# Front blocks' numbers by loads of six registers, group 6 loaded behind its own count, and some orders of work changed

## The reference

```python
x = x + _L0_xattn_ref(_layernorm(x), ctx, ctx, ...)   # softmax cross attention, 16 heads of 8, 77 keys
x = x + _L0_ffn_ref(_layernorm(x), ...)               # 8 experts, top 2, silu(x W1 + b1) * (x W2 + b2), W3
x = x + _L1_xattn_ref(_layernorm(x), ctx, ...)        # linear attention: softmax of q and k over features
x = x + _L1_ffn_ref(_layernorm(x), ...)               # 8 experts, top 2, gelu(x W1 + b1) W2, plus 2 shared experts
```

## Time and profile before

| what | value |
|---|---|
| median of 3 runs | 716.31 us (714.04 to 717.26) |
| profiled execution | 716.5 us |
| its span | 714.5 us |
| PE busy | 655.3 us (92%) |
| DVE, POOL, ACT busy | 452.1, 383.2, 340.4 us (63, 54, 48%) |
| mean DMA rate | 128 GB/s; 250 to 278 GB/s in most of the two routed parts |
| stages | attention 0 to about 243; routed 0 from 260 to 387; attention 1 to 558; routed 1 from 559 to 697; tail to 714.5 |

### The profile page before, as it was taken

How to read it: one execution, slowest core, us unless ns; L and a number is a source line. 1 busy time by engine, 2 the same in 40 slices (tenths; PEclk the granted TensorE clock), 3 DMA queues, 4 the chain that set the end, 5 groups by cost and what they waited for, 6 DMA issues and landing times.

```text
span 714.5 us, 15805 instructions
## 1 busy us (share of the span) xinstructions
PE 655.3 (92%) x5160; PEld 494.1 (69%) x5160; DVE 452.1 (63%) x1336; ACT 340.4 (48%) x739; POOL 383.2 (54%) x502
## 2 busy tenths in 40 slices
PE   6999999999998879999998899999998799999991
PEld 3556666665667669899997455556554599999990
DVE  2577788788877757786778568776564133333433
ACT  3444454454443244444666466766543354544440
POOL 5312255765746744555677566676645145545552
PEclk9999999999999689999999999999999999999997
DMA  6831112112210167888882300000001888888875
GB/s 178 238 61 11 8 20 30 34 19 29 36 26 24 55 174 220 248 260 265 253 262 84 100 31 27 23 30 27 31 21 52 237 272 261 264 261 268 278 232 165
DMA packets 102120, 91.36 MB, mean 128 GB/s; under 512 B 52952, under 2 KB 85848, under 8 KB 101720
## 3 DMA queue, kind: packets, MB, share of 16 engines
q1 hardware_dynamic: 88487, 69.85, 35.4%
q0 software_dynamic: 8640, 17.84, 7.1%
q10 hardware_dynamic: 4913, 2.67, 1.4%
HBM read 69.14 MB, written 22.72 MB: 129 GB/s over the span
## 4 chain that ended last, share of the span: by engine, by line
PE 65%; DVE 14%; SPq 5%; issue 5%; ACT 4%; DMA 3%; POOL 2%; POOLq 0%; DVEq 0%; ACTq 0%
PE pair L1543 37%; PE pair L1877 11%; PE pair L1546 8%; PE pair L1941 5%; DVE sm L1272 4%; DVE smax L1268 4%; PE pair L1668 2%; PE pair L1683 2%; DMA xr<-xs_sorted 1%; SPq L500 1%; SPq L504 1%; POOL xs_sorted L615 1%; SPq L493 1%; ACT L924 1%; SPq L494 1%
## 5 line engine op out<-in xcount | busy, mean ns | idle before, releaser
L689 POOL DMA_INDIRECT y_tok<-ysb,xr x142 | 138.8, 978 | 123.7 <-DVE ysb L1149 58.5
L615 POOL DMA_INDIRECT xs_sorted<-xa,slot_i x128 | 131.5, 1027 | 86.2 <-DVE slot_i L1055 50.9
L1543 PE MATMUL pair<-xT,w_all 128*128 128x256 f32 (+1 forms) x640 | 139.3, 362 | 0.0
L1543 PEld LDWEIGHTS pair<-xT,w_all 128*128 128x128 f32 x640 | 109.7, 196 | 9.6
L1877 PEld LDWEIGHTS pair<-w_all,hT 128*128 128x128 f32 x852 | 107.6, 194 | 6.0 <-issue 2.8
L1877 PE MATMUL pair<-w_all,hT 128*128 128x128 f32 x852 | 109.3, 277 | 2.2 <-DVE hT L1135 1.9
L873 ACT ACTIVATE hT<-pair,w_all 128x256 f32<-128x256 f32 (+1 forms) x160 | 62.5, 448 | 74.5 <-PE pair L1543 73.8
L1127 DVE COPY xT<-pair 128x256 f32<-128x256 f32 (+1 forms) x80 | 31.4, 393 | 95.2 <-PE pair L1546 91.5
L937 ACT ACTIVATE hS<-pair,w_sh 128x512 f32<-128x512 f32 x64 | 44.0, 687 | 60.5 <-PE pair L1543 59.7
L1543 PE MATMUL pair<-xeT_all,w_sh 128*128 128x512 f32 x128 | 68.6, 619 | 0.0
L1941 PE MATMUL pair<-hS,w_sh 128*128 128x512 f32 x128 | 66.4, 602 | 0.0
(11 more groups left out here) (222 smaller groups left out, 1090.3 us busy)
## 6 DMA issues: line engine op xcount, KB each, us to landing
w_all<-in_w SPq DMA_DIRECT2D x40, 578.0 KB, 4.3
w_all<-in_w SPq DMA_DIRECT2D x40, 450.0 KB, 3.9
xa<-y_tok SPq DMA_DIRECT2D x32, 256.0 KB, 4.3
xr<-xs_sorted SPq DMA_DIRECT2D x62, 130.0 KB, 3.3
y_tok<-ysb,xr POOLq DMA_INDIRECT x142
xs_sorted<-xa,slot_i POOLq DMA_INDIRECT x128, 2.3
xs_sorted<-in_pads SPq DMA_DIRECT2D x12, 130.0 KB, 3.9
xr<-xs_sorted SPq DMA_DIRECT2D x18, 65.0 KB, 2.6
```

Source lines behind the costliest of these rows:

```text
L615: g.indirect_dma_start(xs_dram[l], bass.IndirectOffsetOnAxis(ap=slot_i[:, i:i + 1], axis=0), xa[:, GT * c + j // TOPK, j % TOPK, :], None)\
L689: g.indirect_dma_start(y_dram[l], bass.IndirectOffsetOnAxis(ap=xr[u % NXR][:, t, P:P + 1].bitcast(I32), axis=0), ysb[u % NYB][:, t, :], None)\
L1543: return mm(out_, l_, r_, start=True, stop=True)
```

## The change

SP reads several numbers with one instruction: eight tail addresses, the first five experts, the first six rows and counts, and the four counts of a group. SP issues all eight tails. A second row of counts is made for group 6 (`NDYN` = 2), and its results are loaded behind it. In layer 1 the last group's low half is loaded by SP and its high half by ACT. ACT's order in layer 0's blocks becomes up(u), gate_rows(u - 2), beside(u). In attention 1 step 1 spends ten indices of shared half steps instead of eight; there out_turned and project of group 1 come earlier and ranks last; in step 8 shared_turn goes behind list_order. DVE adds a bias ahead of three shifts of the context. The semaphore `lg_ready0` also counts layer 1's logits now, as `lg_ready`.

```diff
 def shared_step(u, k):
-    at = (k if k % 2 else k // 2) if u == 1 else 16 * (u - 1) - 8 + k
-    return divmod(at, 2) if u > 1 or k % 2 == 0 else (-1, 0)
+    at = 16 * (u - 1) - 6 + k
+    if u == 1:
+        at = {0: 0, 1: 1, 2: 2, 3: 3, 4: 4, 5: 5, 8: 6, 9: 7, 12: 8, 13: 9}.get(k, -1)
+    return divmod(at, 2)
...
-                def block_weights(u):
+                def block_weights(u, e=None):
                     after(sp, S("y_sum"), u - NWB + 1)
-                    e = sp.value_load(e_i[0:1, 0, u - u0:u - u0 + 1], min_val=0, max_val=E - 1)
+                    if e is None:
+                        e = sp.value_load(e_i[0:1, 0, u - u0:u - u0 + 1], min_val=0, max_val=E - 1)
...
-                for k in range(0, E - 3):
-                    tail_rows(k)
+                _, ends = nc.values_load_multi_w_load_instructions(tail_i[0:1, 0:E], engines=[sp.engine], min_val=0,
+                                                                   max_val=(E - 1) * PITCH + NTOK)
+                for k in range(E):
+                    sp.dma_start(xs_dram[l][bass.ds(ends[k], P), :], a["pads"][k * P:(k + 1) * P, :])\
+                        .then_inc(S("xs_padded"), 16)
                 sp.wait_ge(S("emap"), l + 1)
                 sp.wait_ge(S("blocks_padded"), 16 * 2 * -(-SPARE // BLK))
+                _, first_e = nc.values_load_multi_w_load_instructions(e_i[0:1, 0, 0:NWB], ...)
+                _, first_r = nc.values_load_multi_w_load_instructions(e_i[0:1, 1, 0:AHEAD], ...)
+                _, first_n = nc.values_load_multi_w_load_instructions(e_i[0:1, 2, 0:AHEAD], ...)
                 for k in range(AHEAD):
                     if k < NWB:
-                        block_weights(u0 + k)
-                    block_rows(u0 + k)
+                        block_weights(u0 + k, first_e[k])
+                    block_rows(u0 + k, first_r[k], first_n[k])
...
-                if l:
+                for g in range(G_READ, G_READ + NDYN if l else G_READ):
+                    if g == G_READ:
+                        sp.wait_ge(S("low_set"), 1)
+                    _, counts = nc.values_load_multi_w_load_instructions(low_i[g - G_READ:g - G_READ + 1, :], ...)
                     for k in range(NYB):
                         sp.wait_ge(S(f"y_out{k}"), counts[k])
-                    results(l, G_READ)
+                    results(l, g)
                 for k in range(NYB):
                     sp.wait_ge(S(f"y_out{k}"), landed(u1, k))
-                for g in range(G_READ + l, NGRP):
-                    results(l, g)
+                for g in range(G_READ + NDYN * l, NGRP):
+                    half_results(sp, l, g, 0)
+                    if l == 0:
+                        half_results(sp, l, g, 1)
...
                 if l == 0:
                     for u in range(NB + 2):
-                        beside(u)
+                        if u < NB:
+                            up(u)
                         if u >= 2:
                             gate_rows(u - 2)
-                        if u < NB:
-                            up(u)
+                        beside(u)
...
             routed(1)
             for g in range(G_STORED, NGRP):
+                if g == U_LAST - 1:
+                    for k in range(NYB):
+                        act.wait_ge(S(f"y_out{k}"), landed(2 * NB, k))
+                    half_results(act, 1, U_LAST, 1)
                 act.wait_ge(S("combined"), NGRP + g + 1)
                 stored_group(act, g)
...
-                for g in range(5, NGRP):
-                    context_shift(g)
                 dve.wait_ge(S("bv_done"), 2)
                 dve.wait_ge(S("bias_in1"), 16 * 3)
                 v.tensor_tensor(bias[:, 5, :], bank[5][:, 0:P], bias[:, 5, :], ALU.add).then_inc(S("bias1_ready"), 1)
+                for g in range(5, NGRP):
+                    context_shift(g)
...
                     fill(6, 7)
                     if u > 1 and live(u):
                         values(u)
+                    if u == 1:
+                        out_turned(u)
                     fill(8, 9)
                     if u == 1:
-                        out_turned(u)
+                        project(u)
                     if live(u - 1):
                         after(pe, S("sx_added"), u - 2)
                         column_sums(1, u - 1)
                     fill(10, 11)
                     if u > 1 and live(u):
                         out_turned(u)
-                    if u == 1:
-                        project(u)
-                    if live(u - 1):
+                    if u > 1 and live(u - 1):
                         ranks(1, u - 1)
                     fill(12)
                     if u > 1 and live(u):
                         project(u)
-                    if live(u - 2):
+                    if live(u - 2) and u != NGRP:
                         shared_turn(u - 2)
                     fill(13)
                     if u == NGRP:
                         list_order(1)
+                        shared_turn(u - 2)
                     fill(14)
                     if u == NGRP:
                         list_smalls(1)
                     fill(15)
+                    if u == 1:
+                        ranks(1, u - 1)
```

More of the change, by code:

```diff
@@ L188 @@
 G_READ = 5
+NDYN = 2
 G_STORED = 4
@@ L321, in build @@
         at2 = sb("at2", [P, NB], BF16)
-        read_by = sb("read_by", [P, 1], BF16)
+        read_by = sb("read_by", [P, NDYN], BF16)
         late = sb("late", [P, 1], BF16)
         row_at = sb("row_at", [1, NB])
-        upto = sb("upto", [1, NB])
-        low = sb("low", [1, NYB])
-        low_i = sb("low_i", [1, NYB], I32)
+        upto = sb("upto", [NDYN, NB])
+        low = sb("low", [NDYN, NYB])
+        low_i = sb("low_i", [NDYN, NYB], I32)
         e_i = sb("e_i", [1, 3, NB], I32)
@@ L539, in routed @@
                             stored_group(sp, g)
[L540 to L543, removed]
-                        counts.append(sp.value_load(low_i[0:1, i:i + 1], min_val=16, max_val=2 * 16 * 2 * NQ))
-                if l:
+                for g in range(G_READ, G_READ + NDYN if l else G_READ):
+                    if g == G_READ:
+                        sp.wait_ge(S("low_set"), 1)
+                    _, counts = nc.values_load_multi_w_load_instructions(low_i[g - G_READ:g - G_READ + 1, :], engines=[sp.engine],
+                                                                         min_val=16, max_val=2 * 16 * 2 * NQ)
                     for k in range(NYB):
                         sp.wait_ge(S(f"y_out{k}"), counts[k])
-                    results(l, G_READ)
+                    results(l, g)
                 for k in range(NYB):
                     sp.wait_ge(S(f"y_out{k}"), landed(u1, k))
-                for g in range(G_READ + l, NGRP):
-                    results(l, g)
+                for g in range(G_READ + NDYN * l, NGRP):
+                    half_results(sp, l, g, 0)
+                    if l == 0:
+                        half_results(sp, l, g, 1)
             def results(l, g):
-                for c, name in ((0, "low_in"), (1, "high_in")):
-                    r = c * NTOK + g * GT * P
-                    sp.dma_start(xa[:, GT * g:GT * (g + 1), c, 0:P],
-                                 y_dram[l][r:r + GT * P, :].rearrange("(t p) d -> p t d", p=P))\
-                        .then_inc(S(f"{name}{g}"), 16)
+                for c in range(TOPK):
+                    half_results(sp, l, g, c)
             routed(0)
@@ L849, in attention0 @@
                 context_values(3)
-                for k in range(E - 3, E):
-                    tail_rows(0, k)
                 for g in range(1, NGRP):
@@ L1588, in list_found @@
                                                 (late[:], late[:]))):
-                    o_ = list_bank(l)[0:1, 64 + k * NB:64 + (k + 1) * NB]
+                    o_ = list_bank(l)[0:NDYN if k == 3 else 1, 64 + k * NB:64 + (k + 1) * NB]
                     mm(o_, by1, at1[:], start=True, stop=False)
@@ L1695, in expand @@
                     if u != U_LAST:
-                        after(pe, S("lg_ready0"), u)
+                        after(pe, S("lg_ready"), u)
                     for t in range(GT):
```

50 lines of the change are left out of this document (25 added, 25 removed).

## The result

| | before | after |
|---|---|---|
| median of the runs | 716.21 us (4 runs, 714.04 to 717.26) | 739.76 us (4 runs, 737.57 to 741.10) |
| profiled execution, its span | 716.5, 714.5 | 739.25, 737.2 |
| mean granted clock of TensorE | 0.966 | 0.956 |

The ratio is 1.033 with a 95% interval of 1.0294 to 1.0365: slower by 3.3%. I had forecast 725.7 and a range up to 730. The sign was right, the size was not.

What follows compares the result with a forecast made beforehand. TensorE, busy 92% of the span, was taken as the bound, so only its waits count: 716.5 + 6.7 (ScalarE's order) + 1.7 (clock) + 1.4 (step u = 1) - 0.6 (starts) + 0 + 0 = 725.7 us. Own range 721.5 to 729; with rivals 713 to 730.

Steps and rivals of the forecast that it cites:

- The two half steps saved at the other end: Layer 1's attention: the shared half steps saved at its far end lie beside SP's work, 0.
- ScalarE's order: Layer 0's routed part, steps 29 to 39: attention work waits for ScalarE, which now does silu and gates first; 6.7 lost.
- The four stalls of 0.84: Layer 0, steps 30, 33, 36 and 37: TensorE waits 0.84 each for a ScalarE copy; 3.4 together.
- the norm's and the Exp's: Layer 0: step 29's wait for the norm adds 1.6, step 32's for the Exp and its table load 1.7.
- Rival 3: Layer 0, steps 29 to 37: ScalarE's new order is free, its copies ending before TensorE's down; starts gain; 711.0; chance 0.17.
- The clock: Layer 0's steps with new idles of 1.9 and 2.15: one stretch at half clock, 1.7 lost, ends 0 and 3.4.
- Step u = 1: Attention of group 1: out_turned's copy and VectorE's residual come later behind two more half steps; 1.4 lost, -0.5 to 1.5.
- The starts: Start of each routed part, where SP is late with rows: layer 0 gain 0, layer 1 gain 0.6.
- The block of 5.2: SP ahead of the first DMA: three loads at 0.31 and 17 checks at 0.25, 5.2 us.
- Rival 1: Starts: cheap loads without the 17 checks, 1.2 more in layer 0 and 3.2 in layer 1; 721.3; chance 0.22.
- Rival 2: Starts and tails: each register as dear as a load, 3 + 2.6 + 1.9 more; 733; chance 0.07.
- The tail: Layer 1's end: the high half leaves earlier but the low half keeps its place; 0, between 0.6 gain and 0.7 loss.

Runs made afterwards that it cites:

- experiments 2: Changed kernel with the shared half steps back at their old places: 725.70 us, ratio 1.0136.
- 3: Changed kernel with ScalarE emptying the shared expert's output ahead of its last pair of gelu halves, not behind: 729.80 us, ratio 1.0216.
- experiments 7: Kernel before with only the new phase of the shared half steps: 729.96 us, ratio 1.0184.
- experiment 6: Kernel before with only ScalarE's new order in layer 0's routed part: 720.99 us, ratio 1.0047.
- experiment 11: Kernel before with the list's order and layer 1's bias moved, first weights issued ahead of row numbers, experts' and rows' checks left out: 712.72 us, 0.9957.
- 12: Changed kernel with ScalarE's order, half-step phase, loads and tails undone, and step 1's out_turned, project and ranks back too: 714.29 us, 0.9983.
- 1: Changed kernel with ScalarE's old order back in layer 0's routed part: 735.18 us, ratio 1.0275.
- 5: Changed kernel with ScalarE's order, the phase of the shared half steps, and the front's and tails' loads all undone: 718.16 us, ratio 1.0021.
- 9: Kernel before with only list_order ahead of shared_turn and layer 1's bias ahead of the context shifts: 713.97 us, ratio 0.9988.
- 10: Kernel before with only the loads of several registers with their checks, and all eight tails on SP: 721.52 us, ratio 1.0101.
- experiment 8: Changed kernel without range checks on experts, rows and tails' ends, the counts' checks kept: 730.68 us, ratio 1.0193.
- experiment 4: Changed kernel with front numbers and tails' ends loaded one by one again, three tails back on ScalarE: 729.36 us, ratio 1.0196.

## Why the prediction was wrong

**The step that failed** is a half sentence, "The two half steps saved at the other end lie beside SP's work: 0". The shift by two half steps was priced in step u = 1, where the extra ones go, and at the far end, where they are saved. But every group from 2 to 8 was shifted, and in each the order against ScalarE's own list changed, which the diff doesn't show since ScalarE's lines there are as they were. Had I laid TensorE's half step 9 against ScalarE's own sequence (norm, gelu, evacuation) in one middle group, the wait was to be read from the trace before. What the runs showed in place of the 0 is a wait of 1.45 for the evacuation of the shared output in each of steps 2 to 8. In steps 3 to 8 it costs 10.1 us, shown by experiments 2 (undone: as before), 3 (one activation moved: 5.9 back) and 7 (alone: the same 10.1).

**What was right by mechanism** is ScalarE's order, 4.5 of the 22.7. Alone it makes the kernel slower by 0.5% (experiment 6), so the sign was not luck, but most of the loss came from terms that the sum had at nothing.

**ScalarE's order:** the mechanism, the places and the sign were right, 6.7 was 4.5. The four stalls of 0.84 are 0.4, since the second silu starts before TensorE's `up` is over by the model of its end; the norm's and the Exp's were 1.3 and 1.7. Rival 3's condition (ScalarE's copy there before TensorE's down ends) was not met once.

**The clock:** no stretch at half clock came in steps 29 to 41, where I put 1.7. Nor did the two of 3.4 us come that the kernel before has there and in step 1 (at 386.5 and 400.1). It came in step 2 and at layer 1's start, behind idles of 3.48 and 6.51 that I hadn't foreseen. The row that I had read it from was no rule either: the idle of 1.93 or 1.94 in front of down(39) stands in eight of the traces, and half clock followed within 3 us in four (before, experiments 7, 11 and 12) and not in the other four (1, 5, 9 and 10).

**Step u = 1:** 1.4 forecast, on the ground that group 1's residual comes later. It starts 20.03 behind block 39 in both kernels, and the product that needs group 1's rows 31.00 behind it in both: 0.0. But with the moved steps TensorE idles ahead of that product, for 3.45 to 3.49 in all seven kernels that have them, and half clock is there in each. In the kernel after this clock took 2.9 of the 3.4 lost in step 2, and it was not in the sum.

**The starts:** 0 and -0.6 forecast, +2.2 and +3.5 found. The block of 5.2 was 6.9: the checks were right (17 x 0.25), the loads not (0.31 each forecast as the nearest row; 0.55 to 0.86 found, 1.2 more for three), and gaps of 0.5 were left out. And rows took longer from their issue to TensorE than the rows that I took it from: block 1's 4.5 in layer 0 (3.4 forecast) and 5.1 in layer 1 (3.9). The spread of layer 0's stretch over kernels without the new front is 111.1 to 113.1 (108.71 in experiment 11), so the 2.2 is good to about 1; the four other kernels with this front have 111.96 to 115.08 (experiment 8, without its checks, 111.30). In layer 1 my sum ended too early: it took TensorE's work behind the first rows at one stretch of half clock, "as now". The idle of 6.51 in front of block 0's rows, where there was none before, left the first up products at 1.92. Rival 1's picture (no checks) was the right lever: experiment 8 gives it.

Rival 2 took each register to be as dear as a load. Here, from SBUF, five registers take 0.55 and six 0.73 or 0.86: 0.07 to 0.12 for each beyond the first (0.27). The dear part was the check. The Trainium skill (Runtime: NRT & Kernel Launch, Instruction fetch mechanics) has about 200 ns per register even in bulk, for loads from HBM; by these rows that doesn't carry over to SBUF.

**The tail:** 0 forecast, 0.2 found. Over all traces it is 24.2 to 24.8 with the old tail (six kernels, mean 24.5) and 24.8 to 25.4 with the new (eight, mean 25.0): the kernels with the halves on two queues have a tail 0.5 longer, not shorter. No kernel had this part alone, so that the queues are the cause is not shown; in the kernel after the low half landed last, 5.56 behind SP's last wait for the scatters, where before it landed 5.32 behind.

## What to carry to other kernels

When a filler is moved in a loop of groups, lay one middle group of every engine side by side and look at each shared buffer's last reader and next writer; the ends of the loop are not where the cost is. Of several numbers loaded together, count the checks, and keep the block of loads behind the first DMA that needs only one of them. A gain of the front can be worth more than its own time where TensorE idles ahead of it, because of the clock behind the idle (experiment 8: 3.7 us earlier, 5.8 us gained). And when an order of work is changed, measure to an instruction that the change leaves where it was.

## What was not expected of the hardware

A load of several registers from SBUF is cheap: 0.55 us for five (0.65 and 0.72 in experiment 8), 0.72 to 0.86 for six, against 0.27 for one; its check is a register operation of 0.147, an assertion of 0.018 and gaps, 0.25 together, for every register. The granted clock is not a fixed part of a kernel: with the same instructions and the same idles in front, step 2 took 22.64 in one kernel and 23.78 in another (experiment 4 and the kernel after), and step 1 22.13 to 23.51 in the kernels that have it as before.
